# Orders and due times of a macaron block's attention stage: a load at another due time, two gate/up products issued on their own

## The reference

```
x = x + 0.5 * ffn(layernorm(x))
x = x + attention(layernorm(x))
x = x + 0.5 * ffn(layernorm(x))
```

## Time and profile before

| | |
|---|---|
| median of 3 runs | 900.36 us (899.62 to 901.2) |
| the profiled execution's own time | 901.34 us |
| its span, first to last instruction | 899.6 us |
| mean granted clock of PE in it | 0.981 |
| busy: PE, DVE, ACT, POOL | 820.8, 631.6, 507.1, 539.3 us |
| stages: first ffn, attention's start, inside, end | 0 to 306, 306 to 350, 350 to 600, 600 to 636 us |
| shared units, change to the experts, second experts, results | 636 to 672, to 700, to 845, to 900 us |

### The profile page before, as it was taken

How to read it: one execution, slowest core, us unless ns; L and a number is a source line. 1 busy time by engine, 2 the same in 40 slices (tenths; PEclk the granted TensorE clock), 3 DMA queues, 4 the chain that set the end, 5 groups by cost and what they waited for, 6 DMA issues and landing times.

```text
span 899.6 us, 26468 instructions
## 1 busy us (share of the span) xinstructions
PE 820.8 (91%) x8310; PEld 752.9 (84%) x8310; DVE 631.6 (70%) x2171; ACT 507.1 (56%) x1321; POOL 539.3 (60%) x650
## 2 busy tenths in 40 slices
PE   4778988999999977999999999997998999999998
PEld 3668887989999976788788888875998999999998
DVE  5775554777777566777778777775575877777497
ACT  5643421666666436776767668665433666666432
POOL 3475652666776416767889888776422576677300
PEclk9798999999999999999999999999999999999999
DMA  7872223544544433334446432163405355555493
GB/s 217 260 239 75 79 84 120 149 131 128 138 134 123 145 48 47 48 50 95 106 74 135 113 63 78 45 154 113 166 26 157 111 157 170 156 155 154 144 371 101
DMA packets 74739, 113.82 MB, mean 127 GB/s; under 512 B 9456, under 2 KB 57776, under 8 KB 73456
## 3 DMA queue, kind: packets, MB, share of 16 engines
q1 hardware_dynamic: 50960, 65.98, 25.2%
q0 software_dynamic: 23648, 46.17, 19.5%
HBM read 59.85 MB, written 52.26 MB: 125 GB/s over the span
## 4 chain that ended last, share of the span: by engine, by line
PE 30%; POOL 12%; issue 11%; ACT 5%; DVE 3%; DMA 3%; SPq 1%; DVEq 0%; another core or an unknown queue 0%; POOLq 0%; ACTq 0%
POOL expert_out L993 8%; PE PSA L1666 7%; PE PSA L1687 4%; PE PSA L1742 4%; POOL YIDX L988 3%; PE PSA L1543 3%; PE PSA L1719 2%; PE PSA L1711 2%; PE PSA L1724 2%; PE PSA L1733 2%; ACT MEM L1162 2%; PE PSA L1567 1%; PE PSA L1505 1%; ACT MEM L1175 1%; PE PSA L1674 1%
## 5 line engine op out<-in xcount | busy, mean ns | idle before, releaser
L993 POOL DMA_INDIRECT expert_out<-MEM,YIDX x142 | 148.8, 1048 | 99.8 <-ACT MEM L1135 97.1
L968 POOL DMA_INDIRECT expert_rows<-MEM,POSU x128 | 130.5, 1019 | 80.9 <-issue 33.5
L1609 PE MATMUL PSA<-EGUh,MEMR 128*128 x568 | 172.5, 345 | 6.1 <-issue 3.4
L1543 PE MATMUL PSA<-MEMR,SGUh 128*128 128x256 f32 x720 | 150.7, 294 | 1.9 <-issue 1.7
L1543 PEld LDWEIGHTS PSA<-MEMR,SGUh 128*128 128x128 f32 x720 | 117.1, 187 | 4.3 <-issue 3.9
L1609 PEld LDWEIGHTS PSA<-EGUh,MEMR 128*128 128x128 f32 x568 | 102.6, 188 | 9.9 <-issue 9.1
L1103 ACT ACTIVATE MEM<-PSA 128x256 f32<-128x256 f32 (+1 forms) x96 | 36.3, 382 | 125.9 <-PE PSA L1543 54.8
L1543 PE MATMUL PSA<-MEMR,SGUl 128*128 128x256 f32 x360 | 103.3, 287 | 0.9 <-issue 0.9
L1298 DVE TENSOR_TENSOR MEM<-PSA,MEM 128x256 f32<-128x256 f32 (+1 forms) x96 | 39.9, 418 | 75.5 <-ACT MEM L1103 43.4
L1609 PE MATMUL PSA<-EGUl,MEMR 128*128 x284 | 91.7, 323 | 0.0
L1122 ACT ACTIVATE MEM<-PSA 128x176 f32<-128x176 f32 x142 | 45.1, 318 | 73.9 <-PE PSA L1609 51.8
(11 more groups left out here) (189 smaller groups left out, 2345.4 us busy)
## 6 DMA issues: line engine op xcount, KB each, us to landing
MEM<-expert_rows SPq DMA_DIRECT2D x142, 130.0 KB
rows_turned<-EGUl SPq DMA_DIRECT2D x7, 1024.0 KB, 4.9
MEMR<-rows_turned SPq DMA_DIRECT2D x14, 512.0 KB, 5.9
X<-expert_out POOLq DMA_DIRECT2D x12, 512.0 KB, 5.9
X<-in_L_attn_x SPq DMA_DIRECT2D x8, 512.0 KB, 6.2
X<-in_L_attn_bo POOLq DMA_DIRECT2D x8, 512.0 KB, 9.6
expert_rows<-FILL SPq DMA_DIRECT2D x30, 130.0 KB
expert_out<-MEM,YIDX POOLq DMA_INDIRECT x142
```

The lines of the kernel that those rows point to most:

```text
L968: pool.indirect_dma_start(out=rows_d[n.f], out_offset=bass.IndirectOffsetOnAxis(ap=POSU[:, k, i:i + 1], axis=0), in_=XN[n.xn][:, c, :], in ...
L993: pool.indirect_dma_start(out=y_d[f], out_offset=bass.IndirectOffsetOnAxis(ap=YIDX[:, j % 8:j % 8 + 1], axis=0), in_=YS[j % 3], in_offset= ...
L1543: last = mm(t[0:h, w * HALF:(w + 1) * HALF], SGU[b][:, w, k, j * P:j * P + h], XT[slot][a][:, k, hf * HALF:(hf + 1) * HALF], start=i == 0, ...
L1609: last = mm(t[:, 0:2 * HE], XGR[j % 2][a][:, k, :], EGU[b][:, bass.ds(e, 1), k, :], start=i == 0, stop=i == 3 * KD - 1)
```

## The change

The two tables of due times and `UNITS` get other numbers. What follows from them for the order of the list, by sorting the due times:

- `state` stands behind `wo_turn` and `turn`, in front of `values`; `wo` of chunk n-1 in front of `back` of n and `scores` of n+1 (before: behind both); `beta` in front of `state` and `values` (before: behind `scores`, in front of `wo`); `decay` behind `back` and `scores` (before: between `values` and `back`); `rturn` directly behind `rout`, one `wo_turn`, `turn`, `state`, `values` earlier.
- On ACT `wo_copy` stands in front of `beta_tanh`; on DVE `beta_decay` behind `state_sum` and `decay_read` behind `attend`.
- The ten units of the first ffn in attention's start stand closer, and all of them with their flush in front of group 0's `xt` (before: seven).
- Group 7's routing steps stand one or two units earlier among the 14 units.

A unit is split into `begin`, PE's gate/up, and the rest; the two first units of the second ffn have their `begin` at 31.53 (behind `values` 31, in front of `wo` 30 and `back` 31) and at 32.6 (behind `wo_turn` 31, in front of `wo` 31). ACT's and DVE's part of a unit is the step `gated` now, at the unit's old place. The load of group 0's rows has the due time 28 in place of 30.

```diff
@@ -106,19 +106,20 @@
 
 
 PLAIN_SUMS = (0, 1)
-WHEN = dict(first_sum=-9.09, scores=-0.12, mask=0.21, select=0.34, turn_copy=-0.15, back=0.88, attend=1.2, proj=-1.99, rope=-1.53, v_copy=-1.51, rope_sum=-1.02,
-            turn=-0.5, values=0.52, ocopy=0.92, wo_turn=1.48, wo_copy=1.61, state=0.34, phi_exp=-1.02, state_sum=0.51, state_scale=1.016, state_wide=1.21,
-            wo=1.937, phi=-0.8, wo_add=2.36, tile_stats=-8.46, tile_stats2=2.518, sum=-11.646, bias=-0.24, stats=-5.43, power=-4.84, scale=-4.66, xt=-4.471,
-            xt_copy=-4.08, xt_low=-3.85, beta=-3.09, beta_tanh=-2.69, beta_decay=-2.63, decay=-2.209, decay_read=-2.06)
-WHEN2 = dict(stats=5.66, power=6.06, scale=6.34, xt=6.78, xt_copy=6.95, xt_low=6.61, gap=0.01, rout=7.09, rout_copy=7.45, rturn=7.538, top=7.88, top_tanh=8.19,
-             rank=8.63, place=8.864, scatter=9.93, every=1.08)
+WHEN = dict(first_sum=-9.0, scores=-0.12, mask=0.21, select=0.34, turn_copy=-0.15, back=0.88, attend=1.2, proj=-1.99, rope=-1.53, v_copy=-1.51, rope_sum=-1.02,
+            turn=-0.5, values=0.52, ocopy=0.92, wo_turn=1.48, wo_copy=1.61, state=0.515, phi_exp=-1.02, state_sum=0.56, state_scale=1.0, state_wide=1.21, wo=1.86,
+            phi=-0.8, wo_add=2.36, tile_stats=-8.46, tile_stats2=2.51, sum=-11.6, bias=-0.24, stats=-5.43, power=-4.84, scale=-4.66, xt=-4.36, xt_copy=-4.08,
+            xt_low=-3.85, beta=-2.487, beta_tanh=-2.3, beta_decay=-2.2, decay=-2.05, decay_read=-1.8)
+WHEN2 = dict(stats=5.66, power=6.06, scale=6.34, xt=6.56, xt_copy=6.95, xt_low=6.61, gap=0.01, rout=7.09, rout_copy=7.45, rturn=7.37, top=7.88, top_tanh=8.19,
+             rank=8.63, place=8.62, scatter=9.93, every=1.08)
 FEED = dict(split=-1.732, split_every=0.287, stats=-3.076, power=-2.485, scale=-2.37, half=0.01, xt=-2.073, xt_copy=-2.09, xt_low=-2.06, gap=0.281, rout=-1.365,
             rout_copy=-1.55, rturn=-1.3, top=-1.31, top_tanh=-0.91, rank=-0.71, place=-0.739, scatter=-0.415, every=0.2, unit=-1.254, unit_every=0.276,
             table=3.74, ends=-4.472, slots=-1.883, blank=-1.74, fixed=3.74, held=0.886, held_every=0.187)
 OWN = dict(xt_low1=0.023, xt2=-0.087, rank2=0.211, place2=0.064, place4=-0.267)
 RAMP = (6, 7)
-UNITS = dict(fill=-11.28, fill_every=1.007, after=32.92, after_every=0.26)
+UNITS = dict(fill=-11.28, fill_every=0.66, after=32.92, after_every=0.3)
 AFTER_UNITS = 14
+BEGIN = (31.53, 32.6)
 TAIL = (2, 6, 8, 9, 12, 14, 15, 18)
 RESULTS = (3, 0, 1, 4, 7, 5, 2, 6)
 OVER = 2
@@ -155,6 +156,7 @@
         self.scored = 0
         self.units = 0
         self.downs = 0
+        self.begun = {}
         self.pending, self.unit_key, self.rs, self.xn_turn, self.xn_last = [], [], {}, {}, {}
         self.stage()
 
@@ -219,12 +221,18 @@
     def shared(self, f, g):
         return [lambda hf=hf, j=j: self.unit(f, g, hf, j) for hf in range(2) for j in range(3)]
 
-    def unit(self, f, g, hf, j):
-        m = self.units
+    def begin(self, f, g, hf, j):
+        m = self.begun[f, g, hf, j] = self.units
         self.units += 1
         self.take(("gu", f, g, hf, j), "GU")
         self.add("gate_up", f, g, SLOT_OF[f][g], hf, j, m)
         self.unit_key.append(("gu", f, g, hf, j))
+
+    def unit(self, f, g, hf, j):
+        if (f, g, hf, j) not in self.begun:
+            self.begin(f, g, hf, j)
+        m = self.begun[f, g, hf, j]
+        self.add("gated", f, g, hf, j, m)
         self.hidden()
         if len(self.pending) == LAG:
             self.down()
@@ -450,13 +458,15 @@
             on(n + w["place"], lambda r=r: self.add("place", r[0]))
             for c in range(GT):
                 on(n + w["scatter"] + c * w["every"], lambda r=r, c=c: self.add("scatter", r[0], c))
-        for n, g in ((NT - 2, 0), (NT, 1), (NT + 1, 2), (NT + 1, 3)):
+        for n, g in ((NT - 4, 0), (NT, 1), (NT + 1, 2), (NT + 1, 3)):
             on(n, lambda g=g: (self.add("xt_load", g, 0), self.add("xt_load", g, 1)))
         for k, unit in enumerate(fill):
             on(UNITS["fill"] + k * UNITS["fill_every"], unit)
         on(UNITS["fill"] + len(fill) * UNITS["fill_every"], self.flush)
         on(UNITS["fill"] + len(fill) * UNITS["fill_every"], lambda: self.enter("attend"))
         units = [s for g in EARLY for s in self.shared(1, g)]
+        for k, at in enumerate(BEGIN):
+            on(at, lambda k=k: self.begin(1, EARLY[0], 0, k))
         on(UNITS["after"], lambda: self.enter("feed"))
         for k, unit in enumerate(units[:AFTER_UNITS]):
             on(UNITS["after"] + k * UNITS["after_every"], unit)
@@ -1091,7 +1101,7 @@
                 a(xn[:, :, D + 3], GTH[:, :], ACT.Copy, scale=0.25, bias=0.25)
                 a(SGC[:, tiles], SGT[:, :], ACT.Copy, scale=0.25, bias=0.25).then_inc(s_wt, 1)
 
-            def gate_up(f, g, slot, hf, j, m):
+            def gated(f, g, hf, j, m):
                 h = HJ[j]
                 t = ready(act, ("gu", f, g, hf, j))
                 if f == 1 and m == first_unit:
@@ -1180,7 +1190,7 @@
                     ready(act, ("wo", n - 1))
                 a(YT, t[:, 0:D].rearrange("p (k t) -> p k t", k=KD), ACT.Copy).then_inc(free(("wo_turn", n)), 1)
 
-            run(plan, {"split": split, "scale": scale, "xt_copy": xt_copy, "top_tanh": top_tanh, "rout_copy": rout_copy, "gate_up": gate_up, "hidden": hidden, "mask": mask, "ocopy": ocopy, "expert_x": expert_x, "expert_up": expert_up,
+            run(plan, {"split": split, "scale": scale, "xt_copy": xt_copy, "top_tanh": top_tanh, "rout_copy": rout_copy, "gated": gated, "hidden": hidden, "mask": mask, "ocopy": ocopy, "expert_x": expert_x, "expert_up": expert_up,
                        "expert_turn": expert_turn, "expert_down": expert_down, "beta_tanh": beta_tanh, "phi_exp": phi_exp, "turn_copy": turn_copy,
                        "wo_copy": wo_copy})
 
@@ -1484,7 +1494,7 @@
                 dve.wait_ge(s_boa[n // GT], 16)
                 v.tensor_tensor(X[:, n, :], t[:, 0:D], X[:, n, :], ALU.add).then_inc(free(("wo", n)), 1)
 
-            run(plan, {"split": split, "stats": stats, "xt_low": xt_low, "top": top, "gate_up": gate_up, "hidden": hidden,
+            run(plan, {"split": split, "stats": stats, "xt_low": xt_low, "top": top, "gated": gated, "hidden": hidden,
                        "shared_add": shared_add, "place": place, "ends": ends, "slots": slots, "expert_x": expert_x, "expert_up": expert_up,
                        "expert_turn": expert_turn, "result_sum": result_sum, "first_sum": first_sum, "tile_stats": tile_stats, "beta_decay": beta_decay, "halve": halve, "decay_read": decay_read, "rope": turned,
                        "v_copy": v_copy, "mask": mask, "state_sum": state_sum, "attend": attend, "wo_add": wo_add})
```

## The result

The changed kernel took 911.64 us (median, 909.54 to 913.74) against 900.78 beside it: 1.0118 times before, 95% interval 1.0088 to 1.0148. It is slower by 10.9 us, where the prediction had 896.0, gave slower a chance of 0.20, and had a range that ends at 903. The profiled execution took 909.54 us, its span is 907.8, 8.2 longer than the span before.

A forecast was written before the change was run, and what follows sets the result against it. TensorE was taken as the bound, with only its idle time at attention's start, inside and end to gain; -5.0 + 3.3 - 2.5 - 0.5 + 0.3 = -4.4 on 901.34 gave 896.9, median 896.0, range 889.5 to 903.

The forecast's parts named there:

- the term for the inside: Inside attention: TensorE's reordering saves 7.5 us and costs 2.4, sum -5, bounds -9 and +1.
- (b): Inside, decay chunks: beta in front of state and values, decay behind back and scores; -0.7 each, five times -3.5 us.
- the same 3.6: Attention's start: beta, tanh, scan, decay and projection take 3.6 us as before, projection at 337.0, +2.3.
- (a): Inside: wo of n-1, 1.1 us, in front of back n fills the wait for ocopy, all but one wait being shorter.
- My fear that select would then come late: Inside: less room between scores and values, 1.8 us down to 0.7; 0.1 us in each of 24 chunks, +2.4.
- (c): Inside: rturn directly behind rout waits 0.35 us for ACT's copy, eating most of 0.58; -0.2 times six, -1.3.
- The start: Attention's start: first-FFN units and flush moved ahead of group 0's xt; +3.3 us, bounds 0 and +8.
- half of the 1.0 and 1.4 for the clock: Attention's start: gate and projection at the lower clock after idle would add +1.0 and +1.4 us; half taken.
- The end: Attention's end: wo and early units fill waits of back, -2.5 us, bounds -6 and +1.5; unit 3's bank freed earlier, -0.5.
- Group 7's route: Group 7's routing: transposes two units earlier, rturn waits 0.45 behind its copy; +0.3 us, bounds -1.5 and +1.5.
- The load: xt_load of group 0 due at 28 instead of 30: SyncE's order unchanged, 0 us.
- rival 1: The start decides: xt's 6 us and a lower clock reach the projection, +8; overall +3.5, 904 us; chance 0.20.

The follow-up runs named there:

- p2: Kernel before with only the five gate steps' due times changed (beta, beta_tanh, beta_decay, decay, decay_read), chip A: 1.0279 of before.
- r4: Kernel before with wo and the state steps as changed, plus xt, sum and tile_stats2 moved: 0.9986 of before on chip D, 1.0003 again on chip B.
- r2: Kernel before with wo, the state steps and all five gate steps as changed, chip D: 1.0093 of before.
- r1: Kernel before with wo and the state steps as changed, plus decay and decay_read moved, beta left in place, chip D: 1.0019 of before.
- q1: Kernel before with wo in front of back and the state steps as changed, chip C: 0.9922 of before, median 892.64 us.
- p3: Kernel before with only rturn moved directly behind rout, chip A: 1.0027 of before.
- q4: Changed kernel with only DVE's order altered, wo_add ahead of the mask and decay_read, chip C: 1.0064 of before.
- p4: Kernel before with only the first ffn's ten units and flush in front of group 0's transposes, and first_sum's due time, chip A: 1.0079 of before.
- p5: Kernel before with only state moved behind wo_turn and turn, with state_sum and state_scale, chip B: 0.9974 of before.
- s1: Kernel before with wo and the state steps as changed, the same kernel as q1 run again on chip B: 1.0007 of before.
- p7: Changed kernel with the five gate steps' due times of before, chip B: 1.0046 of before.
- p8: Changed kernel with gate steps, start and rturn as before, leaving wo, state, the two early units and group 7's steps, chip B: 1.0022 of before.
- r3: Kernel before with wo, the state steps and two units begun early, the first one place later, behind the last router tile's transpose, chip D: 0.9993 of before.
- q2: Kernel before with wo and the state steps as changed, plus the second FFN's first two units begun at 31.53 and 32.6, chip C: 0.9977 of before.
- q3: Kernel before with wo and the state steps as changed, plus the steps behind attention (group 7's transposes, place, units every 0.3), chip C: 0.9956 of before.
- p6: Changed kernel with all the inside's orders back (wo, gate steps, rturn, state), start, end and group 7's steps as changed, chip B: 1.0080 of before.

## Why the prediction was wrong, point by point

**The failed step is the term for the inside, -5.0, in its part (b)**: "`beta` and `decay` move" and "per decay chunk -0.7, five times -3.5". I priced the moves by what the idle in front of `back` would lose, and took every moved instruction's output to have room. The measured difference is +8.3. That the gate steps cost instead of gaining is shown twice against a base on the same chip: 1.0279 with wo behind scores (p2), and 1.0107 relative to r4 with wo in front of back (r2). The runs show two things that the term had at nothing. Inside, the projection waits 4.4 us for a bank that `wo_add` frees (after, p2, r1, r2). In the start, where I had the gate chain at "the same 3.6", the new order makes beta to projection 6.6 us in place of 3.7 (r2, r4).

How the +8.3 divides is known only by subtraction across chips. wo and the state steps gave -5.4 (249.4 to 244.0 in q1, chip C), which is what the whole forecast for the inside was; rturn gave +2.6 (p3, chip A); the remaining +11.1 is what is left for the gate steps. q4, which removed the bank wait, has 4.8 less; beta waiting for the rope is 1.1; the rest I can name only as PE's short waits in front of `values` (3.4 us, where the list of before has none of that kind) and have not shown its cause. The subtraction is weak: moved alone, the same gate steps cost the inside 19.6 us on chip A (p2 and p4) and 2.7 on chip D (r2 and r1, r4), and on chip D the bank wait cost nothing (r1).

The Trainium skill's page "Perfetto Trace Analysis", section Optimizing Tensor Performance, says that independent groups of matmuls should go through different PSUM banks, so that the reading of one lies beside the next one's matmuls. The trace agrees and adds what the reader has to do with it: here the kernel does rotate, and three banks deep, and still waits 4.4 us, since a moved step changes which reader stands three takes behind.

**(a) wo in front of back: right on chip A.** Alone 6 us there; `back`'s waits for ACT fell to 1.6 us (358 to 610), from the 10.8 of the earlier trace rows. On chip B the inside did not get shorter by it: 242.0 us without it (p5) and 242.5 with it (s1). My fear that select would then come late (+2.4) did not show as a wait of that size.

**(c) rturn: the wait was foreseen, its price not.** I had 0.35 us against a lost 0.55, so -0.2 each. The waits are 0.4 to 0.5, and `back` keeps 7.0 + 1.7 us of its own: +2.6 in place of -1.3, by one execution, and 1.0027 (0.9999 to 1.0055) by the times.

**The start: the stretch near, the way different, the price too low.** +3.3 forecast, +2.1 measured at scores 0 (from the first sum to scores 0: 35.1 before, 38.1 after, +3.0). But the edits of the start alone cost 6 us (p4), and I had nothing for them behind scores 0. The sum has a slip too: half of the 1.0 and 1.4 for the clock is 1.2, which makes +3.5. But xt came at 325.24, 3.4 us earlier than I had it, and the gate at 330.19, even 0.9 ahead of before. What brought the loss back is the gate chain, 3.66 us before, 4.92 after, and the clock. PE's timeline and two windows (granted clock third from the end), which answer to the earlier trace rows:

```profile
325.24 1.91 PE L1515 MATMUL PSA<-CN,MEM 128*128 128x128 f32 x8
330.19 1.93 PE L1650 MATMUL PSA<-MEMR,G 128*32 128x128 f32 x32 [3.04 <-DVE MEMR L1261]
334.15 0.44 PE L1657 MATMUL PSA<-CN,MEM 128*128 128x128 f32 x1 [2.03 <-DVE MEM L1428]
```

```profile
325.00:334.00 9.00, 4.08 (x43) 3.25 (x41) 5.58 (x12) 1.84 (x4) 1.31 (x1) 0.50 0.73 111
334.00:348.00 14.00, 9.22 (x41) 7.52 (x45) 5.54 (x21) 6.24 (x12) 6.24 (x6) 0.74 0.04 6
```

The granted clock is 0.50 from 325 to 334, which is the level of 1.2 GHz, and 0.74 in the window behind it, so part of that is at 1.2 GHz too. The eight transposes at 325.24 took 1.91 us, where eight took 1.07 in group 7's row above, so the clock was down before the wait of 3.04 began; TensorE had idled 1.69 us in front of its last down product, at 324.21. Beta took 1.93 in place of 1.08. I had taken half of that cost; by these rows it is nearer the whole. The Trainium skill's page "TensorE: Matmul & The Clock Gate", Part 1, has the throttled state as the default, which activity releases; the trace agrees, with its 1.93.

**The end: -2.5 and -0.5 forecast, -3.3 measured to the last wo**, and +1.2 behind it. The sign is right for a reason that I had only half. From scores 28 to the last wo, 40.8 before and 37.5 after, wo and the state steps alone have 38.0 (q1), rturn alone 41.2 (p3). With the units begun early, rturn in front of values has 35.9 (p7) and the old place 39.1 (p8), on one chip, though p7 has the changed start too. The first unit, which I counted as hidden, is not: the units cost 2.0 to 4.3 us up to the last wo (r3, p8, q2). On chip C the routing on DVE ahead of `attend` is part of that chain, which I left out. On chips B and D there is hardly a wait in front of the last `back` to hide a unit in: where the trace of before has 2.93 us, one of the ten traces has 0.5 (p5) and the other nine have none. Behind the last wo the units gave back 2.6 us in q2 and 1.0 in r3 (259.8 against 260.7), more than the 0.5 forecast, though in the changed kernel the first silu's table load stands at 644.12, right behind the last wo, as before.

**Group 7's route:** +0.3 forecast, +2.3 by the medians (q3), outside my bounds of 1.5 but not clear of noise.

**The load: right.** SP's queue has it at 596.28 behind group 5's store, with group 6's store at 630.52, as in the earlier trace rows.

```profile
595.87 0.32 SPq L887 DMA_DIRECT2D rows_turned<-EGUl  x1
596.28 2.85 SPq L905 DMA_DIRECT2D MEMR<-rows_turned  x2
630.52 0.32 SPq L887 DMA_DIRECT2D rows_turned<-EGUl  x1
```

**Of the rivals** the time is beyond rival 1's 904, and not by its mechanism: the start stayed near +3. None of the rivals had the gate steps as a cost, or the reuse of a bank. The place of that wait could have been read from the kernel before: three banks, the order of the takes, and the DVE queue behind `scores`.

**What would be faster.** wo and the state steps without the rest took 892.64 us, 0.9922 (0.9887 to 0.9957) of before, on chip C; on chip B it is a tie, 1.0007. On C the changed kernel's variant q4 took 905.95. The changed kernel itself had 1.0118 where it ran.

**Open:** what makes wo and the state steps worth 0.8% on one chip and nothing on another. Part of it stands in the traces: the wait that wo was to fill is shorter on chip B. `back` waits 6.9 us for ACT in p6, which has the inside of before, in place of 10.8, and the same inside takes 244.5 us in place of 249.4. Why ACT is later on the other chips is not known (last section). Open are also the 5 us of the inside that no single wait names, and most of what p4 cost.

## What to carry to other kernels

Where outputs take the next bank in a small ring, list the takes in the order of the writing engine before and after a move, and for each the reader that frees the bank and what stands ahead of that reader on its own queue; a moved step with no data dependence on its neighbours can still put a long queue in front of them. A wait found this way is a lead and not yet a price: the same 4.4 us cost nothing in r1, where other waits of that sum went. Filler work put into a wait is hidden only where the wait is: the one in front of the last `back` was 2.93 us in the trace that the forecast was made from, and 0.5 us or nothing on two other chips. And price each part of a compound change by itself, beside its own base on the same chip: two parts brought the whole gain here on one chip, and the others took it back.

## What the runs showed of the hardware that I had not expected

**The same kernel stands 27 us apart between chips.** The kernel before had medians of 875.7, 877.8, 878.5, 899.1 and 903.0 us. A part of it lies in front of attention, in code that no kernel here alters but for the place of the first sum itself: that starts at 310.57 in the kernel before, at 304.7 to 311.5 in the eight traces of chips A and C, and at 294.0 to 302.4 in the ten of B and D. The last wo to the end took 263.7 to 268.6 us on the slower chips and 259.8 to 262.9 on B and D. Single instructions do not differ: ACT's half mask took 1.03 us on B and on C (medians of 32 in s1 and q1), GpSimd's select 1.10 on both. So an edit's worth in a kernel of short waits is to be compared within one chip.

**What differs is when an engine starts.** ACT's copy (`ocopy`) of the last chunk began 0.06 us after the end of `values` in all ten traces of chips B and D, and 2.4 to 4.2 us after it in all ten others (before, after, A, C). The same kernel on C (q1, PE and then ACT) and on B (s1, ACT; its `values` is the row at 606.11 above):

```profile
618.92 1.08 PE L1711 MATMUL PSA<-MEM 128*32 128x128 f32 x32 [0.49 <-POOL MEM L1029]
622.40 0.60 ACT L1175 ACTIVATE MEM<-PSA 128x512 f32<-128x512 f32 x1 [3.55 <-remote]
```

```profile
607.25 0.60 ACT L1175 ACTIVATE MEM<-PSA 128x512 f32<-128x512 f32 x1 [1.31 <-PE PSA L1711]
```

In q1 DVE's copy of the logits starts 0.04 us behind that of ACT, also with "remote" in place of an instruction that ended its wait. Over a whole execution ACT's waits whose end the profile puts down to no instruction ("remote" or "issue") sum to 85 to 108 us on before, after, A and C, and to 0.5 us or nothing on B and D. The 2.93 us in front of the last `back`, on which the forecast for the end rested, comes from a start of this kind: ACT's copy began 2.4 us after `values` ended. What holds the engine there no run shows.
